# Opening of a fused patch-embedding and fast-weight attention tower: load order, warm-up products, and a shared scaling

## The reference, cut to what matters

```python
x: (64, 2, 104, 104); gamma, beta: (10, 104, 104); W: (128, 10, 8, 8)
concat = x and four copies of it shifted by 4 pixels in both directions   # 10 channels
normed = (concat - mean) * rsqrt(var + 1e-7)       # one mean and variance per image
y = conv(normed * gamma + beta, W, stride 8) + b   # 13 x 13 patches, 128 features
h = [cls_tok, y]                                   # 170 tokens per image
q, k, v = layernorm(h) @ Wq.T, Wk.T, Wv.T
for each token t:  S = S + 0.01 * v_t^T k_t (summed over the 64 images);  out_t = S q_t
h = h + out
result = h + layernorm(h)                          # the last block adds the feed-forward's output
```

## Time and profile before

| | us |
|---|---|
| median of 3 runs (lowest, highest) | 217.61 (217.36, 217.68) |
| the profiled execution | 217.46 |
| span of the profiled execution, first to last instruction | 215.6 |
| PE busy in it | 196.3 (91%) |
| POOL, DVE, ACT busy | 154.5, 152.3, 127.7 |

### The profile page before, as it was taken

How to read it: one execution, slowest core, us unless ns; L and a number is a source line. 1 busy time by engine, 2 the same in 40 slices (tenths; PEclk the granted TensorE clock), 3 DMA queues, 4 the chain that set the end, 5 groups by cost and what they waited for, 6 DMA issues and landing times.

```text
span 215.6 us, 5028 instructions
## 1 busy us (share of the span) xinstructions
PE 196.3 (91%) x1548; PEld 166.9 (77%) x1548; DVE 152.3 (71%) x758; ACT 127.7 (59%) x306; POOL 154.5 (72%) x129
## 2 busy tenths in 40 slices
PE   0699999999999999999999999999999999999720
PEld 0488897886888889788888888899888888888610
DVE  3639694684486675678687597687687687699892
ACT  4215777884443375475756565665665574577982
POOL 1069908899990999969999949938999541455671
PEclk9999999999999999999999999999999999999975
DMA  5999992745022006153053432022012012100356
GB/s 140 388 420 422 422 413 112 217 185 181 0 58 111 2 3 194 30 175 88 3 153 109 125 93 49 5 50 49 11 41 52 16 36 52 28 22 5 80 118 152
DMA packets 17216, 25.90 MB, mean 120 GB/s; under 512 B 1719, under 2 KB 13693, under 8 KB 17062
## 3 DMA queue, kind: packets, MB, share of 16 engines
q1 hardware_dynamic: 16486, 25.41, 36.5%
q10 hardware_dynamic: 704, 0.17, 0.4%
HBM read 19.65 MB, written 5.92 MB: 119 GB/s over the span
## 4 chain that ended last, share of the span: by engine, by line
PE 52%; POOL 15%; DMA 10%; DVE 8%; issue 7%; SPq 4%; ACT 2%; POOLq 0%; DVEq 0%; ACTq 0%
PE conv L575 25%; DMA images<-x_rows 10%; PE vr_ps L623 10%; POOL scaled L469 7%; PE first_ps L633 6%; PE outs L650 6%; POOL rstd L1337 3%; PE turn L608 3%; POOL g_low L1327 2%; DVE state L1007 2%; DVE state L999 2%; SPq L488 1%; PE conv L583 1%; DVE images L1028 1%; POOL rstd L1353 1%
## 5 line engine op out<-in xcount | busy, mean ns | idle before, releaser
L575 PE MATMUL conv<-scaled,wt 128*128 128x256 f32 (+3 forms) x432 | 111.7, 375 | 7.3 <-DMA wt<-weight 6.9
L469 POOL TENSOR_TENSOR scaled<-rows,gam 128x832 f32<-128x832 f32 (+1 forms) x54 | 84.7, 1588 | 17.6 <-DMA rows<-x_windows 17.3
L575 PEld LDWEIGHTS conv<-scaled,wt 128*128 128x128 f32 x432 | 71.7, 193 | 15.3 <-DMA wt<-weight 6.9
L817 ACT ACTIVATE values<-vr_ps,rstd 128x256 f32<-128x256 f32 x76 | 36.0, 473 | 62.8 <-PE vr_ps L623 50.1
L1337 POOL TENSOR_TENSOR rstd<-var,powers 128x8 f32<-128x8 f32 (+2 forms) x20 | 30.3, 1517 | 27.0 <-DVE var L1019 26.9
L999 DVE TENSOR_TENSOR state<-first_ps,state 128x128 f32<-128x128 f32 x76 | 22.1, 291 | 27.6 <-PE first_ps L633 22.2
L825 ACT ACTIVATE images<-images,ln_shift,ln_gain 128x128 f32<-128x128 f32 x80 | 37.3, 489 | 1.5 <-DVE ln_shift L1076 0.7
L623 PE MATMUL vr_ps<-w_high,g_low 128*128 128x256 f32 x77 | 30.8, 400 | 0.8 <-ACT values L817 0.8
L1327 POOL TENSOR_TENSOR g_low<-g_t,g_high 128x512 fp32r<-128x512 f32 x21 | 26.8, 1274 | 4.6 <-ACT g_high L804 4.6
L988 DVE BATCH_NORM_STATS2 ln_stats<-images 128x6 f32<-128x128 f32 x85 | 23.6, 284 | 4.8 <-ACT images L811 4.7
L1007 DVE TENSOR_TENSOR state<-second_ps,state 128x128 f32<-128x128 f32 x76 | 21.5, 282 | 2.1
(11 more groups left out here) (201 smaller groups left out, 273.5 us busy)
## 6 DMA issues: line engine op xcount, KB each, us to landing
rows<-x_windows SPq DMA_DIRECT2D x12, 864.0 KB, 4.8
out<-images SPq DMA_DIRECT2D x40, 128.0 KB, 2.4
images<-x_rows SPq DMA_DIRECT2D x4, 832.0 KB, 14.9
images<-x_rows SPq DMA_DIRECT2D x1, 1040.0 KB, 15.9
images<-x_rows SPq DMA_DIRECT2D x1, 624.0 KB, 20.7
rows<-x_windows SPq DMA_DIRECT2D x1, 448.0 KB, 6.1
gam<-gamma SPq DMA_DIRECT2D x1, 422.5 KB, 6.8
bet<-beta SPq DMA_DIRECT2D x1, 422.5 KB, 9.0
```

Source lines behind the costliest of these rows:

```text
L469: return eng.tensor_tensor(scaled[:, s, at + skip:at + N], window[:, skip:N], gains.unsqueeze(2).to_broadcast([P, N - skip, B]), ALU.mult)
L575: last = pe.matmul(conv_ps[g % 2][:, at:at + n * B], held, scaled[:, s, a % RING:a % RING + n], start=first, stop=(g < EARLY and s >= TOP ...
L817: act.activation(values[:, t % VALUE_SLOTS].rearrange("p a e -> p (a e)"), vr_bank(t)[:, 0:2 * E], ACT.Identity, scale=rho_of(t)).then_inc ...
```

## The change

- **Zero products.** PE opens with three products of the tile `zeros` (512 columns each, into a bank whose contents are not used) and puts a fourth behind shift 0 of group 0.
- **Row 0 by parts.** DVE scales the first eight tokens of all four shifts of row 0 first, then the other five tokens of each.
- **Row 1 shared.** DVE scales the first three tokens (13 to 15) of all five shifts of row 1, and POOL the other ten, so 192 and 640 elements per partition instead of POOL's 832. New counter `scaled_second`.
- **Order on PE.** The table of gamma comes before that of beta, and shifts 0 and 1 of group 1 come between the two.
- **Row 3 ahead.** SP loads row 3 ahead of image parts 5 and 6; for this it waits, in front of these three, for all eight parts of DVE's row 0.
- **Group 4 by halves.** Its ten pieces are taken as the first halves (tokens 32 to 35) of all five shifts, then the second halves. Five stand before the image sums, four behind them, one behind L755's product; two pieces of group 5 follow there (`AHEAD`), and `FIRST` begins with 4 instead of 2. Nothing of group 4 is left behind the `early` products.
- **Low parts.** DVE's subtraction for `picks` products comes after image part 0, not after part 1; row 4's load waits also for `scaled_second`.

```diff
-FIRST = (2, 2, 1, 1, 1, 1, 1, 1)
+AHEAD = 2
+FIRST = (4, 2, 1, 1, 1, 1, 1, 1)
+SECOND = 2 * TOKENS
...
         def wait_scaled(eng, s, a, n):
             last = (a + n - 1) // N
             if a // N == 0:
-                eng.wait_ge(scaled_first, s + 1)
+                eng.wait_ge(scaled_first, s + 1 if a < TOKENS else TOP + 1 + s + 1)
...
+            elif 0 < last and a + n <= SECOND:
+                eng.wait_ge(scaled_second, s + 1)
...
+                if r == ROW_SLOTS:
+                    sp.wait_ge(scaled_second, SHIFTS)
...
             load_images(4)
+            sp.wait_ge(scaled_first, 2 * (TOP + 1))
+            load_row(3)
             load_images(5)
             load_images(6)
-
-            sp.wait_ge(scaled_first, TOP + 1)
-            load_row(3)
             load_row(4)
...
+            def conv_fifth(a, z):
+                items = conv_items(EARLY - 1)
+                for item in (items[0::2] + items[1::2])[a:z]:
+                    conv(item)
...
+            def zero_products(count):
+                for _ in range(count):
+                    pe.matmul(vr_ps[:, 0:PER_GROUP * E], zeros[:], zeros[:].unsqueeze(1).to_broadcast([P, PER_GROUP, E]),
+                              start=True, stop=True, skip_group_check=True)
+
+            pe.wait_ge(zeros_ready, 1)
+            zero_products(3)
             pe.wait_ge(weight_in, 16)
-            conv_shifts(0, 0, SHIFTS)
+            conv_shifts(0, 0, 1)
+            zero_products(1)
+            conv_shifts(0, 1, SHIFTS)
...
+            pe.wait_ge(gamma_in, 16)
+            table_columns(1, gam)
+            conv_shifts(1, 0, 2)
+            pe.wait_ge(beta_in, 16)
+            table_columns(0, bet).then_inc(columns_done, 1)
...
-            conv_shifts(1, 0, SHIFTS)
+            conv_shifts(1, 2, SHIFTS)
...
             conv_shifts(3, 0, SHIFTS)
+            conv_fifth(0, 5)
             pe.wait_ge(sums_ready, 2)
...
-            conv_shifts(EARLY - 1, 0, 2)
+            conv_fifth(5, 9)
             pe.wait_ge(scale_cols_ready, 1)
...
-            conv_shifts(EARLY - 1, 2, 4)
+            conv_fifth(9, 10)
+            for item in LATE_ITEMS[0:AHEAD]:
+                conv(item)
             pe.wait_ge(own_scales_ready, 1)
...
-            conv_shifts(EARLY - 1, 4, SHIFTS)
...
-                scale_shift(dve, 0, s).then_inc(scaled_first, 1)
+                scale_shift(dve, 0, s, 0, TOKENS).then_inc(scaled_first, 1)
+            for s in range(TOP + 1):
+                scale_shift(dve, 0, s, TOKENS).then_inc(scaled_first, 1)
+            dve.wait_ge(gamma_in, 16)
+            dve.wait_ge(row_in[1], 16)
+            for s in range(SHIFTS):
+                scale_shift(dve, 1, s, 0, SECOND - N).then_inc(scaled_second, 1)
...
-                scale_shift(pool, r, s).then_inc(scaled_rows, 2 if (r, s) == (N - 1, BOTTOM) else 1)
+                scale_shift(pool, r, s, SECOND - N if r == 1 else 0).then_inc(scaled_rows, 2 if (r, s) == (N - 1, BOTTOM) else 1)
```

More of the change, by code:

```diff
@@ L458, in tile_of, with scale_shift @@
             return buf[t // PER_GROUP % slots][:, at:at + E]
-        def scale_shift(eng, r, s):
+        def scale_shift(eng, r, s, first=0, stop=N):
             offsets = (r if s < 3 else r - 1) % ROW_SLOTS
@@ L463, in scale_shift @@
             window = rows[:, r % ROW_SLOTS, 0:N] if s == 0 else rows[:, offsets, right:right + N]
-            skip = 1 if r * N == CORNER else 0
-            gains = gam_first[:, s] if r == 0 else gam[:, s, r * N + skip:r * N + N]
+            skip = 1 if r * N == CORNER else first
+            gains = gam_first[:, s, skip:stop] if r == 0 else gam[:, s, r * N + skip:r * N + stop]
             if (r, s) == (N - 1, BOTTOM):
@@ L468, in scale_shift @@
             at = r % 2 * N
-            return eng.tensor_tensor(scaled[:, s, at + skip:at + N], window[:, skip:N],
-                                     gains.unsqueeze(2).to_broadcast([P, N - skip, B]), ALU.mult)
+            return eng.tensor_tensor(scaled[:, s, at + skip:at + stop], window[:, skip:stop],
+                                     gains.unsqueeze(2).to_broadcast([P, stop - skip, B]), ALU.mult)
         block = ctx.enter_context(nc.Block())
@@ L589, in conv_shifts @@
                         conv(item)
+            def conv_fifth(a, z):
+                items = conv_items(EARLY - 1)
+                for item in (items[0::2] + items[1::2])[a:z]:
+                    conv(item)
             def late_conv(t, half):
-                share = [i for i, st in enumerate(ITEM_STEPS) if st == t]
+                share = [i for i, st in enumerate(ITEM_STEPS) if st == t and i >= AHEAD]
                 mid = (len(share) + 1) // 2
@@ L704, in tail, with table_columns @@
                 reads(LAST + 1)
+            def zero_products(count):
[4 more added lines that the diff above has]
+            zero_products(3)
             pe.wait_ge(weight_in, 16)
-            conv_shifts(0, 0, SHIFTS)
-            pe.wait_ge(gamma_in, 16)
-            pe.wait_ge(beta_in, 16)
-            for kind, table in enumerate((bet, gam)):
+            conv_shifts(0, 0, 1)
+            zero_products(1)
+            conv_shifts(0, 1, SHIFTS)
+            def table_columns(kind, table):
                 for i in range(SHIFTS):
@@ L713, in _ @@
                                      stop=(i == SHIFTS - 1), skip_group_check=True)
-            last.then_inc(columns_done, 1)
+                return last
+            pe.wait_ge(gamma_in, 16)
[3 more added lines that the diff above has]
+            table_columns(0, bet).then_inc(columns_done, 1)
             pe.wait_ge(small_in, 16)
@@ L1260, in _ @@
                         last_stats = dve.bn_stats(stats[:, 2 * j:2 * j + 2].rearrange("p a b -> p (a b)"), part)
+                if i == 0:
+                    for blk, ps in enumerate((turn_ps, second_ps)):
+                        m = P if blk == 0 else PATCHES - P
+                        dve.wait_ge(table_high_ready, blk + 1)
+                        dve.tensor_tensor(term_parts[0:m, blk, :, 1], ps[0:m, 0:2 * E].rearrange("p (k e) -> p k e", e=E),
+                                          term_parts[0:m, blk, :, 0], ALU.subtract).then_inc(table_low_ready, 1)
                 if i == 1:
```

6 lines of the change are left out of this document (1 added, 5 removed).

## The result

| | before | after |
|---|---|---|
| median, us | 217.63 (4 runs, 217.36 to 217.68) | 220.41 (4 runs: 218.50, 219.82, 220.99, 221.18) |
| granted clock, run by run | 0.982 (profiled) | 0.984, 0.976, 0.964, 0.964 |
| profiled execution, us | 217.46, span 215.6 | 218.50, span 216.7 |

The account below looks back on a forecast made before the run. The end was taken as fixed by when the image statistics complete, the time from there to `vr`, and PE's work behind it. 217.46 + (36.9 - 33.34) - 1.0 - 0.86 = 219.2 us; range 216.9 to 220.9.

Parts of the forecast that it names:

- the main case: DVE's row-1 scalings alternate with POOL's, so PE reaches the image-sum product at 36.9: 219.2 us, chance 0.50 including rival 4.
- The collision: In row 1, DVE and POOL each wait for the other's whole instruction: 1.33 us a round, DVE's fifth ending at 18.4.
- The give-back behind the product: Behind the image-sum product, ACT's earlier group copy returns 1.0 us up to `vr`, two fewer PE pieces behind it 0.86.
- The clock: PE's idle from 16.3 to 20.1 drops it to 1.2 GHz, doubling about 3 us of work: 222.3 us, chance 0.11.
- Rival 1: In row 1 DVE isn't held by POOL; PE's lead ends waiting for image sums at 35.4: 217.7 us, chance 0.22.
- Rival 2: DVE isn't held, and PE's queue, not POOL's chain, decides between image sums and `vr`: 216.9 us, chance 0.17.
- Row 3's load: Row 3 ahead of image parts 5 and 6 delays the sums up to 2.1 us, nothing more in the likeliest case.
- The opening: Up to the weight products, faster group 0 and early group 1 shifts give PE 2.1 us of lead, if DVE keeps its times.
- rival 4: In the opening the zeros don't raise the clock; group 0 runs at half speed: 219.2 us, chance within the 0.50.
- DVE's own times: DVE's scalings in rows 0 and 1, start to start: 0.63 us for 512 elements, 0.43 for 320, 0.30 for 192.

Follow-up runs that it names:

- gains in PSUM: The changed kernel, with DVE first copying its 15 row-1 gains into PSUM and reading them there: 218.59 us median of 12 runs, ratio 1.0031.

## Why the prediction was right, and where it was off

The direction was right, and so was the mechanism of the schedule, nearly step by step. The size lies in the range partly by luck: the schedule was forecast to cost 1.7 us (219.2 against 217.46) and cost 1.0 (218.50 in the undisturbed execution), and the clock, which the main case left out, added some 2 to the median. Predicted, then measured in the undisturbed execution:

| step | predicted | measured |
|---|---|---|
| group 0 ends | 11.5 | 11.78 |
| a round of DVE and POOL | 1.33 | 1.33 |
| DVE's fifth ends | 18.4 | 18.62 |
| weight products, `centered` | 20.1 | 20.38 |
| group 2 begins | 25.5 | 25.66 |
| image sums ready | 35.4 | 35.5 |
| **image-sum product** | 36.9 | 36.82 |
| `early(0)` | 41.1 (36.9 + 4.22) | 40.82 |
| `vr` | 53.97 (51.41 + 3.56 - 1.0) | 53.73 |
| time, clock kept | 219.2 | 218.50 |

- **The collision** is what the forecast rested on, read off two instructions near 46 us. That they would alternate, and not that one goes first until it is done, came out to 0.01 us a round. The gains in PSUM show the cause.
- **The give-back behind the product** was the term mis-sized: -1.0 - 0.86 = -1.86 where the traces show 179.9 instead of 182.2 us behind the product, 2.36 less ahead of rounding. Up to `vr` it was 1.16 (18.07 before, 16.91 after), for ACT's copy 1.0 predicted; behind `vr` 1.2, for two pieces 0.86. Counted over PE's queue alone it would have been the five pieces, 2.16. What the rest is, no run isolates. This made the sum 0.5 too high.
- **The clock** was the true miss. I had it as a rival of 0.11 at 222.3, instead of a part of the main case: a wait of nearly 4 us was forecast, and that PE runs at half speed after an idle stretch stood in the earlier trace rows. The mechanism was priced at +3.1; the one profiled fall behind this wait cost 2.56, and the four runs of after lie 0 to 2.7 above the undisturbed one. No row of before showed a fall inside the run, and I took that for evidence; before has no such wait: behind the opening none is over 0.37 us until 1.1 in its tail. So the median came out 1.2 us high while the schedule was 0.7 low, and two of four runs passed the range's upper end.
- **Rival 1** foretold 217.7 for a DVE that isn't held: with the gains in PSUM the product stood at 35.41 (predicted 35.4), and the undisturbed executions took 217.1, less by 0.6, nearly all of it the same mis-sized term. Missing was again that PE waits there, by 2.12 us, and that the clock may fall behind it (median 218.59). Rival 2 needed a DVE that isn't held too. Its sum, which counts the five pieces in full, gave 216.9, and is the nearer of the two to 217.1; its claim that PE's queue decides up to `vr` isn't borne out, as PE waits for ACT's values at `vr` in that trace too, 0.37 us.
- **Row 3's load** was priced at 2.1 us and costs 1.92 on the sums product (35.26 against 33.34) where PE is early, and nothing in the change as made, both as said. Of POOL the prediction said that it gains nothing, which is right, but for 30.4 as the start of its shift 0; it began at 31.48, waiting for PE's products of group 3 with this half of `scaled`, not for the load (30.40, when PE was earlier, named the load).
- **The opening** was priced at 2.1 us of lead. With the gains in PSUM PE reached the sums at 33.29 (35.41 - 2.12) with 2.16 us of group 4 more done, against 33.11 before: 2.0. It could be had only with the share's wait and the load order gone. The zeros raised the clock, about 5 us in, which sank rival 4. Without them PE reaches the sums at 34.33 instead of 33.17 (33.62 less its wait of 0.45), so 1.2 of the 2.0 us are theirs, and 0.7 of that counts in the time.
- **DVE's own times** were reckoned with a fixed 0.1 us for each instruction, which no row of before shows. The scalings of 512, 320 and 192 elements came 0.60, 0.40 and (gains in PSUM) 0.27 us apart, for 0.63, 0.43 and 0.30 predicted: too little to matter.

## What to carry to other kernels

Before work is moved from one engine to a neighbour, look in the trace for any place where the two already run that form together: one pair of stretched instructions gave the price of ten. Here one of DVE's two operands in PSUM took the pairs apart, for one copy of 0.17 us. Price every new wait of TensorE twice, once as time and once as the clock that may fall behind it, and look at the spread of the runs before believing one profile. Edits whose gains and losses meet at the same later point must be tested together and apart: here, of the four parts tried alone, one paid, two lost, the one's loss hiding the other's, and the fourth paid only once these two were undone.

## What the runs showed of the hardware

- Five DVE scalings of 128x192 beside five of POOL of 128x640, all with two SBUF inputs: 1.41 us for each of DVE's but the first, 1.33 from start to start on both. With DVE's gains in PSUM: 0.35 each, 0.27 from start to start, POOL's 1.26 instead of 1.37.
- Around waits of 3.50, 3.20, 2.12 and 1.97 us, executions of one kernel took different times at different mean clocks; with a wait of 1.66 us (zeros alone, 12 runs from 217.32 to 217.96) the runs keep together. Two falls stand in traces: one that began within a wait of 3.49 us cost 2.56 us (granted 0.64 over 7.83 us), one that began 1.1 us behind a wait of 2.12 cost 1.3.
- A granted clock of 1.00 in the opening doesn't mean full speed. Here is the opening of the kernel after, in which the zero products start 1.02, 0.85, 0.85, 0.85 and 0.66 us behind the one ahead; the two at 8.04 start 0.43 apart:

```profile
1.00:6.50 5.50, 4.83 (x6) 1.85 (x6) 2.19 (x11) 3.63 (x2) 0.30 (x8) 1.00 0.74 206
```

The clock stands as 1.00 there, but the trace's record of it has no entry until 5.06 us, within the product whose distance is 0.66, and the views count the time ahead of the first entry as 1.00. In the kernel before the first entry stands at 13.07 us, where the distances go from 0.43 to 0.22. So ahead of the first entry the distances between products are what tells the speed; behind it, in the two falls above, record and distances agree.
